# One-layer perceiver kernel: part of the self-attention weights prepared during the fold and the second tile, first keys and half of the first queries made inside the fold

## The reference

```
x = x + cross_attention(layernorm(x), ctx)      # 16 heads; rope on the context; a low-rank chain of weights
x = x + self_attention(layernorm(x))            # 16 heads of 128; weights = codes * scales (blocks of 32 rows); biases
x = x + moe(layernorm(x))                       # softmax router, top 8 of 64 experts, silu(gate) * up, down
```

## Time and profile before

| | |
|---|---|
| runs | 742.62, 743.28, 745.24 us (median 743.28) |
| profiled execution | 742.43 us, of which the span from first to last instruction is 740.4 |
| busy, share of the span | PE 86%, PE weight load 74%, DVE 61%, ACT 39%, POOL 35% |
| mean granted TensorE clock | 0.929 of full speed (full: 2.4 GHz; the lower level, 0.5, is 1.2 GHz) |
| fold | to 78.2 us |
| hT, kt0, qa, qb of tile 0 | 78.2 to 91.7 us |
| tile 0 | 91.7 to 150.9 us |
| tile 1 | 150.9 to 204.3 us |
| tile 2 | from 204.3 us, some 55 us |

### The profile page before, as it was taken

One profiled execution on the slowest core, in us unless ns is written; L12 is line 12 of the kernel. 1 busy time (PEld: TensorE's weight loads), 2 busy tenths in 40 slices (PEclk: granted clock), 3 DMA queues, 4 the chain that ended last, 5 costly groups with the idle time before them and its releaser, 6 DMA issues.

```text
span 740.4 us, 16762 instructions
## 1 busy us (share of the span) xinstructions
PE 634.2 (86%) x6373; PEld 546.4 (74%) x6373; DVE 453.3 (61%) x1246; ACT 285.9 (39%) x788; POOL 258.7 (35%) x281
## 2 busy tenths in 40 slices
PE   5998576699999998999999999999888879999910
PEld 4887555598788797788798788797777767778900
DVE  1135475556577686777677677677575335555648
ACT  1112365334635634634635635635412033333400
POOL 3202568521121441341441441410404325555620
PEclk9996656699999999999999999999999999999965
DMA  7974799299030230140140110100101759999567
GB/s 197 274 197 112 177 244 226 59 298 296 24 113 3 68 132 2 38 162 3 41 159 2 47 39 2 41 25 2 61 2 47 219 149 330 330 322 305 150 253 298
DMA packets 93503, 100.83 MB, mean 136 GB/s; under 512 B 26560, under 2 KB 84473, under 8 KB 92401
## 3 DMA queue, kind: packets, MB, share of 16 engines
q1 hardware_dynamic: 86672, 83.38, 39.1%
q0 software_dynamic: 6144, 15.96, 5.9%
q10 hardware_dynamic: 608, 0.42, 0.2%
HBM read 65.17 MB, written 36.18 MB: 137 GB/s over the span
## 4 chain that ended last, share of the span: by engine, by line
PE 57%; DVE 18%; DMA 8%; ACT 8%; issue 6%; SPq 2%; POOL 2%; POOLq 0%; DVEq 0%; PEldq 0%; ACTq 0%
PE bank L1452 6%; PE bank L1226 6%; PE bank L1228 6%; PE bank L1227 5%; PE bank L1259 4%; PE bank L1291 4%; DMA Wh<-expert_rows 4%; PE bank L1340 3%; PE bank L1245 3%; PE bank L1461 2%; PE bank L1280 2%; PE bank L1215 2%; PE bank L1443 2%; PE bank L1203 2%; ACT diag L693 2%
## 5 line engine op out<-in xcount | busy, mean ns | idle before, releaser
L655 ACT ACTIVATE pr<-bank,nmax 128x257 f32<-128x257 f32 x128 | 61.3, 479 | 96.1 <-DVE nmax L873 95.7
L1226 PE MATMUL bank<-space,Wh 128*128 128x128 f16 x512 | 88.1, 219 | 0.3
L1228 PE MATMUL bank<-space,Wl 128*128 128x128 f16 x512 | 88.1, 219 | 0.0
L1227 PE MATMUL bank<-space,Wh 128*128 128x128 f16 x512 | 88.1, 219 | 0.0
L533 POOL DMA_INDIRECT expert_rows<-h,slot x64 | 62.9, 983 | 64.7 <-DVE slot L970 48.9
L516 POOL TENSOR_TENSOR Cr<-C,Ct 128x192 f32<-128x192 f32 x64 | 40.7, 658 | 121.1 <-PE bank L1291 110.9
L595 POOL DMA_INDIRECT pair_rows<-Wh,etok x64 | 62.2, 972 | 54.0 <-issue 30.2
L873 DVE TENSOR_REDUCE nmax<-bank 128x1 f32<-128x257 f32 x128 | 53.3, 421 | 43.4 <-PE bank L1273 41.2
L1291 PE MATMUL bank<-Cr,pT 128*128 128x64 f32 x512 | 75.6, 273 | 0.1
L1291 PEld LDWEIGHTS bank<-Cr,pT 128*128 128x128 f32 x512 | 72.2, 204 | 0.2 <-ACT pT L663 0.2
L663 ACT COPY pT<-bank 128x256 f32<-128x256 f32 x128 | 47.5, 371 | 63.1 <-PE bank L1280 61.0
(11 more groups left out here) (191 smaller groups left out, 1526.2 us busy)
## 6 DMA issues: line engine op xcount, KB each, us to landing
expert_rows<-h SPq DMA_DIRECT2D x8, 1120.0 KB, 13.7
Wh<-expert_rows SPq DMA_DIRECT2D x64, 140.0 KB, 3.9
pair_rows<-zrow SPq DMA_DIRECT2D x8, 1024.0 KB, 9.1
Wl<-L_ffn_gate_up_proj_dram SPq DMA_DIRECT2D x36, 192.0 KB, 3.8
ring<-L_ffn_gate_up_proj_dram SPq DMA_DIRECT2D x28, 192.0 KB, 3.7
space<-pair_rows SPq DMA_DIRECT2D x5, 1024.0 KB, 8.9
Wl<-L_ffn_down_proj_dram SPq DMA_DIRECT2D x36, 96.0 KB, 4.7
C<-ctx_dram SPq DMA_DIRECT2D x24, 128.0 KB, 3.8
```

What stands on the lines that cost most here:

```text
L655: e.activation(pr[:, s, :], bank[r % 2][:, 0:NL], ACT.Exp, bias=nmax[:, s:s + 1], accum_out=rsum[:, s:s + 1]).then_inc(expd, 1)
L1226: e.matmul(dst, ah, bh, start=first and n == 0, stop=False)
L1227: e.matmul(dst, ah, bl, start=False, stop=False)
L1228: ins = e.matmul(dst, al, bh, start=False, stop=last and n == len(terms) - 1)
```

## The change

- Parts: `FOLD_PARTS` is (0, 1, 2, 3), so six parts are made in the fold. Tile 0 makes five (rows 1, 4, 7, 10, 13), tile 1 five (rows 1, 3, 4, 6, 7). There is a seventh buffer, and the order of the buffers is written out.
- In the fold DVE's order changes: M copy, statistics, in group 2 also tile 0's h1, then the group's remaining part.
- Tile 0's `hT`, `kt0`, `qa` are made inside group 3 of the fold, in other PSUM banks (`X0_BANK`), and only `qb` after the last M copy. PE's `x_skip` for the three uses behind `qb` moves to r = 2 of tile 0. `fkqT` gets a place of its own, since `qspace` is now written during the fold.
- SP loads context 1 ahead of part 3, and context 2 ahead of part 14.
- PE's self attention of tile 0 (in tile 1) waits for `w_done` 9 before queries and keys and for 12 before values. The bias row is made in one piece at the place of `pos` (r = 12); DVE takes it at r = 13 and adds it at r = 14.
- POOL clears `diag` in tile 1 behind part 12, and ACT waits for that at r = 13.

The diff, cut to its core (moved blocks whose text stays the same are left out):

```diff
-FOLD_PARTS = (0, 0, 2, 3)
+FOLD_PARTS = (0, 1, 2, 3)
...
-TILE_PARTS = dict(zip((0, 2, 3, 5, 6, 8, 9, 11, 12, 14, 15), range(PART0[GROUPS], PARTS)))
...
+TILE_PARTS = ({1: 6, 4: 7, 7: 8, 10: 9, 13: 10}, {1: 11, 3: 12, 4: 13, 6: 14, 7: 15})
...
+NPB = 7
+BUFFER = [0, 1, 2, 0, 1, 2, 3, 4, 5, 6, 0, 1, 2, 6, 0, 1]
...
-        fkqT = qspace[0:QC, :].rearrange("p (h c d) -> p h c d", h=GH, c=2)
+        fkqT = cut(GH * 2 * P, QC).rearrange("p (h c d) -> p h c d", h=GH, c=2)
...
+            diag[:, :, :].rearrange("p a b -> p (a b)"), space[:, 0:2048], space[:, 2048:4096], space[:, 4096:6144],
+            space[:, 6144:8192])]
...
+        X0_BANK = {"hT": 2, "kt0": 3, "qa": 4, "qb": 6}
+
+        def xbank(name, i):
+
+            if isinstance(i, int) and i == 0 and name in XNEXT:
+                return bank[X0_BANK[name]]
+            return XBANK[XS.index(name) % 2]
...
-            for u in range(3, 6):
-                load_part(u)
-
             e.wait_ge(roped, 2 * BT)
             load_context(1)
-            for u in range(6, PARTS):
+            for u in range(3, 14):
+                load_part(u)
+
+            e.wait_ge(roped, 4 * BT)
+            load_context(2)
+            for u in range(14, PARTS):
                 load_part(u)
 
...
 
-                e.wait_ge(roped, i * (2 * BT))
-                load_context(i)
+                if i > 2:
+                    e.wait_ge(roped, i * (2 * BT))
+                    load_context(i)
...
-                    if i == 0:
-                        for r, u in TILE_PARTS.items():
+                    if i < 2:
+                        for r, u in TILE_PARTS[i].items():
                             if RB * b <= r < RB * (b + 1):
                                 part_low(u)
+                                if i == 1 and BUFFER[u] == 2:
+                                    e.wait_ge(w_done, u + 1)
+                                    e.memset(diag[:, :, :], 0.0).then_inc(zeroed, 1)
                     if b == BT - 1 and m is not None:
...
-            e.wait_ge(w_done, PARTS)
-            e.memset(diag[:, :, :], 0.0).then_inc(zeroed, 1)
...
-                        if isinstance(i, int) and i == 0 and r in TILE_PARTS:
-                            part_high(TILE_PARTS[r])
+                        if isinstance(i, int) and i < 2 and r in TILE_PARTS[i]:
+                            part_high(TILE_PARTS[i][r])
+                    if isinstance(j, int) and j == 0 and r == 13:
+                        e.wait_ge(zeroed, 2)
...
-            e.sem_inc(x_high, XSPLIT.index("kt0"))
-            for name in XNEXT:
-                x_use(name, 0)
...
+                if g == GROUPS - 1:
+                    e.sem_inc(x_high, XSPLIT.index("kt0"))
+                    for name in XNEXT[:-1]:
+                        x_use(name, 0)
...
+            x_use(XNEXT[-1], 0)
...
-            e.wait_ge(zeroed, 2)
...
-                    if isinstance(j, int) and j == 0 and r == 4:
+                    if isinstance(j, int) and j == 0 and r == 13:
                         obias_out()
-                    if j is not None and r == 5:
+                    if j is not None and r == (14 if isinstance(j, int) and j == 0 else 5):
                         add_obias(j)
...
+                if g == GROUPS - 1:
+                    for name in XNEXT[1:-1]:
+                        x_low(name, 0)
...
+                if g in (1, 2):
+                    all_stats(g - 1)
+                if g == 2:
+                    next_h1(0)
+                for u in left:
+                    part_mul(u)
+
+            x_low(XNEXT[-1], 0)
...
-            next_h1(0)
-            for name in ("kt0", "qa", "qb"):
-                x_low(name, 0)
...
+                if not (isinstance(i, int) and i == 0 and name == "qb"):
+                    e.wait_ge(xd[bk_], need - 1 + FREE)
...
                 elif name[0] in "qk":
+                    if isinstance(j, int) and j == 0:
+                        e.wait_ge(w_done, 9)
...
                 elif name[0] == "v":
+                    if isinstance(j, int) and j == 0:
+                        e.wait_ge(w_done, 12)
...
+                e.wait_ge(sd[bk_], need - 1 + FREE)
+                e.wait_ge(w_done, PARTS)
+                e.wait_ge(bv_split, 2)
+                split(dst[:, 0:D], [(bvh[:, h:h + 1].to_broadcast([P, P]), bvl[:, h:h + 1].to_broadcast([P, P]),
+                                     Wh[:, 6 + h // 8, (h % 8) * D:(h % 8 + 1) * D],
+                                     Wl[:, 6 + h // 8, (h % 8) * D:(h % 8 + 1) * D]) for h in range(H)]).then_inc(sf[bk_], 1)
...
-                        elif name[:2] == "wo" and isinstance(j, int) and j == 0:
-                            obias_sum(name)
+                        elif name == "pos" and isinstance(j, int) and j == 0:
+                            obias_sum()
...
+                        if isinstance(i, int) and i == 0 and r == 2:
+                            for name in XS[XS.index("qb") + 1:]:
+                                x_skip(name, -1)
...
-            for name in XS:
-                (x_use(name, 0) if name in XNEXT else x_skip(name, -1))
...
+                if g < GROUPS - 1:
+                    rope_transposes(g + 1)
+                else:
+                    for name in XS[:XS.index("qb")]:
+                        (x_use(name, 0) if name in XNEXT else x_skip(name, -1))
+
...
+            e.wait_ge(f_md, GROUPS)
+            e.wait_ge(f_na, GROUPS)
+
+            x_use("qb", 0)
             tile(0, None, None)
```

146 lines of the change are left out of this document (61 added, 85 removed).

## The result

The changed kernel takes 753.45 us (median of 20 executions, 744.39 to 761.81), the kernel before took 744.18 in the same session (20 executions, 736.64 to 756.86): ratio 1.0119, 95% interval 1.0084 to 1.0154, or +9 us (+7.3, ±3.2, by the means of all executions). I had forecast 739.7, with a range to 746.5. It went the other way, and further than the slower rival C.

What follows compares the result with a forecast made beforehand. PE was taken to set the pace from the second token tile on, with tile 0 and the preparation soft. Terms 0 - 18 + 10.4 + 4 = -3.6 from 742.43, plus 0.85, gave 739.7 us; range 733.5 to 746.5.

Steps and rivals of the forecast that it cites:

- rival C: Slower whole kernel: part 15's subtraction in tile 1 ends near 35, opening the gate late; 745.4 or 747.4 us; chance 0.2.
- Fold and preparation, 0: Stretch up to tile 0's first nmax: three PE gaps saved, new waits inside the fold; net 0 (-1 to +2) us.
- wait (1): Fold: ACT's cast of part 0 waits for DVE, delaying the copies for group 2; PE loses 1.5 us.
- Wait (2): Fold group 2: ACT's cast of part 2 delays group 3's copies and h1T; PE stands about 2.3 us before qa.
- Tile 0, -18: Tile 0: fewer parts remove 13.8 us of gaps, clock mostly kept; -18 us (-11 to -21).
- Rival B: Tile 0 stays at 1.2 GHz and gains only 14 us; whole kernel +0.4, 743.7 us, no change; chance 0.25.
- Tile 1, +10.4: Tile 1: bias sum, longer chain, lower clock and added parts lengthen the full tile; +10.4 us (+6 to +14).
- (a): Tile 1: the output bias sum, 48 products moved to row 12, becomes a term of its own; +5.25 us.
- (b): Tile 1 rows 0 to 3: part multiplies and a cast delay the chain to q0, 10.8 after first nmax; +2.9 us.
- (c): Tile 1: PE busy some 3 of the first 11 us, so the clock falls; +2.7 us.
- Head of tile 2, +4: Tile 2's start waits for the blanking of expert_rows, 67.8 us after tile 1's first nmax; +4 us (0 to +7).
- Rival C's port: Tile 1: DVE and POOL share an exclusive SBUF port; five subtractions could block DVE up to 10.6 us, 0.8 counted.

Runs made afterwards that it cites:

- e1: The kernel before, unchanged, profiled a second time: median 745.09 us, ratio 0.999 to the kernel before.
- e2: The changed kernel, unchanged, profiled a second time: median 752.22 us, ratio 1.016 to the kernel before.
- e6: The kernel before, unchanged, profiled a third time: median 736.06 us, ratio 0.9997.
- e13: The kernel before with 24 of 64 experts, the base for the other runs with experts cut: median 665.11 us.
- e16: The changed kernel with tile 1 put back (new fold only, ten parts in tile 0) and 24 of 64 experts: median 673.44 us.
- e14: The changed kernel with 24 of 64 experts: median 678.33 us.
- e17: The changed kernel with stores spread, fold of the kernel before, eight parts in tile 0, three in tile 1: 731.74 us, ratio 1.0005 to the kernel before.
- e5: The changed kernel with the eight blanking stores spread behind the loads of parts 13, 14 and 15: median 739.47 us, kernel before 738.59.
- e7: The changed kernel with tile 1 put back, new fold kept, ten parts in tile 0: 741.17 us, ratio 1.006 to the kernel before.
- e9: The changed kernel with the blanking stores spread, a repeat of e5: 745.73 us, ratio 1.003 to the kernel before.
- e12: The changed kernel with stores spread, seven parts in tile 0 and three in tile 1: 744.84 us, ratio 0.999 to the kernel before.
- e10: The changed kernel, unchanged, profiled a third time: 749.26 us, ratio 1.010 to the kernel before.
- e8: The changed kernel with tile 1's bias sum at row 12 cut from 48 products to 3: one profiled execution, 744.41 us.
- e15: The changed kernel with the blanking stores spread and 24 of 64 experts: median 671.93 us.
- e18: A repeat of e12 (stores spread, seven parts in tile 0, three in tile 1): 734.24 us, ratio 1.001 to the kernel before.
- e3: The changed kernel with all eight blanking stores issued right behind the last weight part's load: 744.34 us, ratio 1.007 to the kernel before.

## Why the prediction was wrong, step by step

**Fold and preparation, 0.** Right where the clock was low, too low where it was high. Profiles whose clock rose at about the same times can be compared (rises in us from the start of the span). First rise at 51 us (e1, e2): first nmax 94.59 and 94.51, so 0, with the last M copy 6 us later (85.99 against 79.95, my "85 to 87") and the preparation 6 shorter. Rises at 14 and 31 us: e6 85.37 against 87.61 after, +2.2; e13 82.07 against e16 84.22, +2.2, and e14 85.28, +3.2, of which 0.9 was there before the wait. Rises at 34 and 47 us: e17, which has neither the head nor part 0 in the new places (though DVE's new order), 88.95 against 88.59 to 90.46 in e5, e7, e9 and e12, -0.4 to +1.5. I had priced wait (1) at 1.5 us of PE; it is 1.4 to 3.2, and in e14 and e16, where the clock was up, it had fallen behind it, which I hadn't counted. Wait (2), priced at 2.3, was 2.0 to 3.1. And I had left only 4.8 to 6.6 us from the end of the last M copy to the first nmax, where it was 7.8 (79.78 to 87.61 in the kernel after): part 5's multiply, below, stands there, with its cast ahead of qb's on ACT, and the bias split took 1.6 us (85.99 to 87.58) instead of 0.3. My sum "91.4 to 93.2" is also narrower than its own terms, which give 89.8 to 93.6.

```profile
79.70 2.69 DVE L827 SCALAR_TENSOR_TENSOR diag<-diag 128x1024 f32<-128x1024 f32 x1
```

All this rests on a few profiles with similar, not equal, clock histories, so 0 to 3 is argued rather than shown.

**Tile 0, -18: the step that failed most.** Tile 0 averages 44.2 us over four profiles of the changed kernel, 56.8 over four of the kernel before: -12.6 (13.7 in the first pair), where I had named less than 13 as a sign of being wrong. Three things were off. The base: 59.2 came from one profile, the longest of the four (53.8 to 59.2). The waits: my -13.8 for gaps and 4 back made -9.8; PE's idle time in the tile fell from 18.6 us to 10.7, by 7.9. And the clock: I wrote "with the clock mostly kept" and took 8 for it; PE's busy time fell by 5.8 (40.6 to 34.8) at a granted clock of 0.75. In e10, at 0.88, PE is idle just as long (10.6) and busy 30.7, which is the whole difference between 45.5 and 41.3. The waits that stayed are behind rows' pT copies and ahead of the out product (kernel after):

```profile
98.91 0.41 PE L1260 MATMUL bank<-ident,pr 128*128 128x128 f32 x2 [2.05 <-ACT pT L662]
...
111.10 0.66 PE L1260 MATMUL bank<-ident,pr 128*128 128x128 f32 x2 [2.25 <-ACT pT L662]
...
126.70 0.41 PE L1235 MATMUL bank<-ident,On 128*128 128x128 f32 x2 [1.70 <-DVE On L878]
```

So "no single wait over 1.6 us" was wrong. Rival B, tile 0 at -14, is close to what came.

**Tile 1, +10.4: right in size.** With the gate out of the way (stores spread) it is 62.5 to 63.8 us against 53.2 to 53.5, or +9 to +10.6. (a) the bias sum 4.6 for 45 of its 48 products (e8), for 5.25; (b) q0 at 11.2 after the first nmax (144.28 against 133.08) for 10.8; (c) the clock: 0.70 in the first 11 us and 0.52 around q0, as these windows of the kernel after show; row 12 comes 33.9 after the first instead of 28.9, so (b) and (c) made 5.0 together where I had 5.6; how it divides between them is open.

```profile
133.10:144.10 11.00, 5.23 (x27) 3.83 (x25) 8.37 (x23) 5.62 (x15) 5.78 (x5) 0.70 0.12 34
137.00:147.20 10.20, 7.06 (x44) 6.01 (x45) 7.01 (x15) 6.58 (x16) 5.64 (x3) 0.52 0.09 18
```

**Head of tile 2, +4: the right mechanism, 3 us too small.** SyncE's first expert load came 29.86 after tile 1's first nmax, for 29.3. From there to DVE's release it was 39.9 us (162.94 to 202.81), for 38.5. The gate opens at 69.7, for 67.8, and without it tile 2 would start 62.5 or 63.2 behind tile 1 (e5, e9), for 63.8: +6.7 to +7.5 for 4.

**Rival C's port.** Its condition, the last subtraction ending near 35, did not occur: 29.9. DVE's multiplies of parts in tile 1 took 1.21 to 1.59, so they lost 0.4; and one normalisation, which takes 0.40 to 0.41 elsewhere, took 1.88 beside a subtraction and ended with it, a loss of 1.5. That makes 1.9 in all, between the 0.8 that I had counted and that rule's bound of 10.6; whether tile 1 took longer for it is not shown. POOL lost 1.0 as well. The pairs, in the kernel after:

```profile
144.38 1.59 DVE L827 SCALAR_TENSOR_TENSOR space<-space 128x1024 f32<-128x1024 f32 x1
...
156.95 1.88 DVE L1001 TENSOR_SCALAR h<-X,mv,rs 128x256 f32<-128x256 f32 x1
```

```profile
144.86 3.11 POOL L559 TENSOR_TENSOR Wl<-diag,Wh 128x1024 f16<-128x1024 f32 x1
...
156.55 2.14 POOL L559 TENSOR_TENSOR Wl<-space,Wh 128x1024 f16<-128x1024 f32 x1
```

A subtraction of 2.12 took 3.11 when it began inside DVE's multiply; behind it POOL had only the memset of diag and then a pause of 0.72, so nothing waited for it. The Trainium skill (SBUF — State Buffer, "SBUF: two separate sides") gives the shared port to whichever starts first, "for the whole instruction"; the trace agrees for this pair (144.38 + 1.59 = 145.97, and 145.97 + 2.12 is within 0.12 of the subtraction's end).

**The sum.** By the profiles: front 0 to 3, tile 0 -12.6, tile 1 with the gate 70.2 - 53.3 = +16.9; together +4.3 to +7.3 where I had -3.6. Of the difference 5.4 is tile 0, 2.5 tile 1 with its gate (16.9 for 14.4), and up to 3 the front. Timed, the four comparisons (+7.3 ±3.2, +9.1 ±3.1, +4.8 ±3.5, +11.2 ±5.8), weighted by their intervals, give +7.6 (±1.8). With the stores spread the three (-1.1, +1.2, +5.1) give +1.3 (±2.2), so 6.3 (±2.8) of the 7.6 goes with the gate. Set side by side in the same comparison, e10 against e9 gave 3.6 (±3.7) and e14 against e15 6.1 (±3.8). For the new fold alone +4.1, +1.6 and +6.2 give +3.2 (±2.2): some 2 of it is tile 0 (58.7 with ten parts against 56.8 with eleven), the rest may be the fold's waits, but e17 and e18 don't tell it from nothing. How much the front costs over many executions could not be measured, since a profile shows one clock history.

My forecast of "faster" had a chance of 0.52 on a clock that I called mostly kept against my own row of 0.65. The profile's own evidence, 1.2 GHz again after each long gap, spoke for rival B, and B comes nearest: its +0.4, with a gate of 69.7 instead of 67.8, tile 0 at -12.6 instead of -14 and an assumed 2 us in front, would be +5.7, at the low end of what was measured.

## What to carry to other kernels

When work moves from one stage into the next, look for whoever waits for its end in program order on a third queue. Here SyncE issued 9 us of expert loads and 21 us of stores behind the last weight part. While that had 22 us to spare it cost nothing; once the part came later than the cover allowed, tile 2 started by the stores and not by tile 1's own work (e8). Bulk stores that depend on nothing should be issued ahead of such a wait: spread among the loads or all at once, both took the wait away, and the times don't tell which is better (+1.2 ±2.8 for e9, +2.7 ±3.8 for e3, over the kernel before). A filler (the bias sum) that stands under a serial chain costs nothing there; moved to a full stretch, it cost its length, and the chain that it had filled ran with PE half idle and the clock at the lower level. A part of weights moved out of a crowded tile is worth what the loads allow: eight parts fitted, ten didn't. And a base read from one profile of a kernel whose executions scatter by 5 us is good to no more than that: profile it twice before subtracting.
